# Attention inside the chunk: two row groups in turns instead of one after the other

## The reference, cut to what matters

```python
def step(S, inp):
    q_t, k_t, v_t, beta_t = inp
    retrieval = jnp.einsum('bhij,bhj->bhi', S, k_t)
    S = S + jnp.einsum('bhi,bhj->bhij', beta_t * (v_t - retrieval), k_t)
    o_t = jnp.einsum('bhij,bhj->bhi', S, q_t)
    return (S, o_t)
```

## Time and profile before

| | us |
|---|---|
| median of 3 runs | 1087.6 |
| lowest and highest | 1085.69, 1088.12 |
| the profiled execution | 1085.21 |
| its span, first to last instruction | 1083.3 |
| mean granted clock of TensorE | 0.927 |

### The profile page before, as it was taken

One profiled execution on the slowest core, in us unless ns is written; L12 is line 12 of the kernel. 1 busy time (PEld: TensorE's weight loads), 2 busy tenths in 40 slices (PEclk: granted clock), 3 DMA queues, 4 the chain that ended last, 5 costly groups with the idle time before them and its releaser, 6 DMA issues.

```text
span 1083.3 us, 19506 instructions
## 1 busy us (share of the span) xinstructions
PE 917.9 (85%) x6091; PEld 697.9 (64%) x6091; DVE 912.3 (84%) x2731; ACT 651.2 (60%) x1574; POOL 478.6 (44%) x667
## 2 busy tenths in 40 slices
PE   7799999999999999999999989899797701796066
PEld 7577887878787787787787776666565500343044
DVE  5789999989999999999999997665676788699887
ACT  4566676657667766666666643556667431695085
POOL 4444464455456545445345352316467550780000
PEclk9899999999999999999999999999999855798579
DMA  9600000000000000003000000214200000000012
GB/s 167 121 5 7 6 11 7 7 7 9 6 6 11 7 6 11 6 6 128 6 7 10 7 7 10 89 59 143 90 1 1 1 0 0 1 1 1 1 59 97
DMA packets 28573, 30.49 MB, mean 28 GB/s; under 512 B 5548, under 2 KB 23864, under 8 KB 28472
## 3 DMA queue, kind: packets, MB, share of 16 engines
q1 hardware_dynamic: 28256, 29.12, 10.5%
q10 hardware_dynamic: 216, 0.14, 0.0%
HBM read 20.85 MB, written 4.19 MB: 23 GB/s over the span
## 4 chain that ended last, share of the span: by engine, by line
PE 71%; DVE 21%; issue 5%; ACT 1%; DMA 1%; SPq 1%; POOL 0%; DVEq 0%; ACTq 0%; POOLq 0%
PE ps L1867 7%; PE ps L1859 7%; PE ps L1798 5%; PE psG L1821 5%; PE psY L1835 5%; PE psX L1835 4%; PE ps L1979 4%; PE psX L1913 3%; PE psY L2000 3%; PE psY L1913 3%; PE psG L1815 3%; PE psX L2000 2%; PE ps L1927 2%; PE ps L2165 2%; PE psG L1979 2%
## 5 line engine op out<-in xcount | busy, mean ns | idle before, releaser
L521 POOL TENSOR_TENSOR arena<-arena 128x256 f32<-128x256 f32 x32 | 23.3, 729 | 308.5 <-DVE arena L1147 300.9
L626 ACT ACTIVATE arena<-ps 128x512 f32<-128x512 f32 x128 | 72.9, 596 | 39.8 <-PE ps L1859 39.4
L1859 PE MATMUL ps<-work 32*128 32x256 f32 x512 | 93.7, 405 | 3.3 <-ACT work L672 2.3
L489 POOL TENSOR_SCALAR_AFFINE_SELECT arena<-arena 128x2048 f32<-128x2048 f32 x32 | 92.1, 2880 | 2.2
L591 ACT ACTIVATE arena<-ps,nparity 32x256 f32<-32x256 f32 x124 | 51.2, 459 | 48.7 <-PE ps L1798 48.3
L1859 PEld LDWEIGHTS ps<-work 32*128 32x128 f32 x512 | 62.2, 186 | 20.3 <-issue 12.5
L1821 PE MATMUL psG<-arena 128*128 128x512 f32 x128 | 73.2, 657 | 0.0
L1158 DVE TENSOR_TENSOR arena<-arena 128x256 f32<-128x256 f32 (+1 forms) x96 | 66.8, 696 | 3.3
L1798 PE MATMUL ps<-work,arena 128*128 128x64 f32 x496 | 63.2, 283 | 6.7 <-DVE work L1173 6.6
L1161 DVE TENSOR_REDUCE arena<-arena 128x64 f32<-128x256 f32 (+1 forms) x96 | 65.9, 687 | 3.3
L1835 PEld LDWEIGHTS psY<-work,arena 128*128 128x128 f32 x512 | 58.7, 192 | 12.6 <-DVE arena L1230 11.6
(11 more groups left out here) (349 smaller groups left out, 2604.3 us busy)
## 6 DMA issues: line engine op xcount, KB each, us to landing
arena<-in_mask_BxSxS_ik SPq DMA_DIRECT2D x8, 1024.0 KB, 7.2
xs<-arena SPq DMA_DIRECT2D x256, 16.0 KB, 1.8
arena<-in_ctx SPq DMA_DIRECT2D x8, 512.0 KB, 4.2
out<-xs SPq DMA_DIRECT2D x32, 128.0 KB, 1.7
arena<-in_x SPq DMA_DIRECT2D x8, 288.0 KB, 16.8
arena<-in_L_ffn_w SPq DMA_DIRECT2D x2, 1024.0 KB, 22.7
arena<-in_x SPq DMA_DIRECT2D x16, 96.0 KB, 5.7
arena<-in_L_attn_w_qkvb SPq DMA_DIRECT2D x2, 512.0 KB, 4.5
```

Source lines behind the costliest of these rows:

```text
L489: G.affine_select(out=pairs, in_=pairs, compare_op=ALU.is_ge, fill=0.0, base=0, pattern=[[0, NH], [-CT, B], [0, CT]], channel_multiplier=1 ...
L626: A.activation(attn[j % 2][:, r * 512:(r + 1) * 512], ps[(2, 0)[r % 2]][:, :], ACT.Copy).then_inc(att_out, 1)
L1859: last = M.matmul(ps[(2, 0)[r % 2]][:, f * 2 * P:(f + 1) * 2 * P], kq[j % 4][rows, f * P:(f + 1) * P], qe[rows, f].rearrange("p e t -> p ( ...
```

## The change

`attention` is now called once per pair of groups, `attention(j, f)` with pair 0 (groups 0 and 1) and pair 1 (groups 2 and 3). Inside, f is the outer loop and the two groups the inner one, so that the matmuls alternate between groups and banks. The waits of a pair all stand before its first matmul: `ust_ready` is waited for before group 0 also, and pair 1 waits until both evictions of pair 0 are done. Each group still raises `att_mm` after its last matmul.

```diff
-            def attention(j, r):
-                if r == 0:
+            def attention(j, pair):
+                if pair == 0:
                     pe.wait_ge(qe_ready, j + 1)
                     if j >= 1:
                         pe.wait_ge(x_done, j - 1)
-                elif r == 1:
                     pe.wait_ge(ust_ready, j)
                 else:
-                    pe.wait_ge(att_out, 4 * j + r - 1)
-                rows = slice(32 * r, 32 * r + 32)
+                    pe.wait_ge(att_out, 4 * j + 2)
                 for f in range(DC):
-                    last = M.matmul(ps[(2, 0)[r % 2]][:, f * 2 * P:(f + 1) * 2 * P], kq[j % 4][rows, f * P:(f + 1) * P],
-                                    qe[rows, f].rearrange("p e t -> p (e t)"), start=True, stop=True)
-                last.then_inc(att_mm, 1)
+                    for r in (2 * pair, 2 * pair + 1):
+                        rows = slice(32 * r, 32 * r + 32)
+                        last = M.matmul(ps[(2, 0)[r % 2]][:, f * 2 * P:(f + 1) * 2 * P], kq[j % 4][rows, f * P:(f + 1) * P],
+                                        qe[rows, f].rearrange("p e t -> p (e t)"), start=True, stop=True)
+                        if f == DC - 1:
+                            last.then_inc(att_mm, 1)
...
                 for f in range(2):
                     if exists(j):
-                        attention(j, 2 * f)
-                        attention(j, 2 * f + 1)
+                        attention(j, f)
```

## The result

| | before | after |
|---|---|---|
| median, us | 1086.4 of 20 runs | 1090.8 of 20 runs |
| lowest and highest | 1079.25, 1090.91 | 1084.01, 1092.65 |
| the profiled execution | 1085.21 | 1091.96 |
| its span | 1083.3 | 1090.1 |
| mean granted clock of TensorE | 0.927 | 0.925 |

The ratio of after to before is 1.0032, with a 95% interval of 1.0018 to 1.0046: 3.5 us more, between 2.0 and 5.0. The means of the two sets of 20 runs, 1086.2 and 1089.7, differ by the same 3.5. The change makes the kernel slower by a third of a per cent.

The account below looks back on a forecast made before the run. TensorE's unbroken line was taken to set a steady chunk's time. The wait's 1.9 us plus 0.5 in chunk 31 gave 2.4, so 1087.6 for the profiled execution and 1090.0 on the median; range 1087.0 to 1092.6.

Parts of the forecast that it names:

- Part 1: Attention matmuls in turns: row groups already run side by side, so the new order gains nothing and costs zero.
- Part 2: The ust_ready wait ahead of group 0 becomes its own instruction: 0.08 us later per chunk, 1.9 us over 24 chunks.
- The upper bound of 0.08: First pair's delay per chunk, bounded 0.01 to 0.08 us; the top assumes the load starts 0.11 after L608 ends.
- The bare shift: Group 0 losing its 0.60 us head start in the first pair: nothing, since group 1 set the pair's end; 0.01 per chunk.
- Part 3: Second pair waits for both evictions: covered, by 0.05 us only, by far gram and turned norms; costs where cover is missing.
- Chunk 31: Last chunk, nothing between the pairs: second pair's later group starts 0.54 us late; carried as 0.5, bounds 0.1 and 1.1.
- A: Rival, 4%: first pair shrinks to the second's form, 0.59 us in 24 chunks, 14.2 in all: 1073.4.
- B: Rival, 16%: the ust_ready wait ahead of the first pair is free; 0.7 us left, 1088.3, no measurable change.
- C: Rival, 9%: cover between the pairs fails, second pair starts 0.07 us late in 24 chunks: 1.7 more, 1091.7.
- D: Rival, 11%: idling before the first pair lowers TensorE's clock, 1.6 us a stretch: one fall 1091.6, every fifth chunk 1098.

Follow-up runs that it names:

- e9: The kernel before with VectorE's solve step t = 8 left out from chunk 1 on: ratio to before 0.9895, chunk 20.213 us.
- e4: The changed kernel with ust_ready named in the middle of the three waits and x_done last: ratio to before 1.0038, chunk 20.262 us.
- e5: The changed kernel with a fourth, long-met wait (k_ready) named last, making two wait instructions: ratio to before 1.0070, chunk 20.413 us.
- e1: The changed kernel's alternating matmuls, but each group's wait stays ahead of its own first matmul as before: ratio to before 1.0014, chunk 20.207 us.
- e2: The kernel before, matmuls still group by group, but with the waits of the change: ratio to before 1.0021, chunk 20.320 us.
- e3: The changed kernel with ust_ready named first of the three waits, so it rides on the weight load: ratio to before 1.0000, chunk 20.213 us.
- e7: The changed kernel with both halves of the far gram moved behind the second pair: ratio to before 1.0382, chunk 21.10 us.
- e6: The kernel before with both halves of the far gram moved behind the second pair: ratio to before 1.0103, chunk 20.545 us.
- e8: The kernel before with the far gram's first half ahead of the first pair, the second between the pairs: ratio to before 1.0004, chunk 20.184 us.
- e11: The kernel before with the retrieval's first two waits exchanged, so ScalarE's sexp_act is named first: ratio to before 0.9997, chunk 20.196 us.

## Why the prediction was right, and where it wasn't

Predicted were 1090.0, a range of 1087.0 to 1092.6, and slower as the likeliest. The ratio gives 1087.6 × 1.0032 = 1091.1, and the median of after is 1090.8. That 1090.0 lies only 0.8 under it is partly luck: the predicted difference of 2.4 was 1.1 under the measured 3.5, and the median of three runs that it was added to was 1.2 above the median of 20.

**What bounds the kernel.** Right: e9 shortens VectorE and the steady chunk doesn't move, while what is added ahead of the first pair comes out in the chunk within 3 ns: against group 1's 808 ns in before, attention starts 46, 91 and 197 ns later in e4, after and e5, and the chunk grows by 49, 94 and 200.

**Part 1, turns cost and bring nothing.** Right, by e1: 20.207 against 20.213. The Trainium skill's page "TensorE: Matmul & The Clock Gate" (Part 3, "The mechanism") has matmuls start and end in strict program order. The prediction set against it, but these are weight loads and don't settle how matmuls go. The matmul records do. In the second pair of before, and in both pairs of e2, all four records of one group stand ahead of the other's in the program, and yet the later group's first starts 13 or 14 ns after the earlier group's first. In the first pair of before, group 0's last record starts 147 ns after group 1's first (each group's records are told by their spacing of 216 ns). Here the trace and the page part. In turns (e1) the groups start 7 ns apart, and the pair takes the same 1.13 or 1.14.

**Part 2, the form of the wait.** Right in mechanism, and close in size. The load comes 0.11 after L608's end, as the earlier trace rows had it, and that it is the form and not the wait is shown by e3, e4 and e5: 0.05, 0.07, 0.11 and 0.22 us for the same release, by how it is named. The text left open whether `ust_ready` would share an instruction with `x_done`. It does, and still costs 0.11, while the earlier trace rows and e4 have 0.07 for such an instruction. The difference is which of the two is named last: in after it is the late one, in e4 and the earlier trace rows a fulfilled one. That the condition named last is looked at first, so that `x_done` has still to be gone through in after, would fit, and so do the 2.6 us of e4's wait instruction against 51 ns in after; no run shows the inside of that instruction. Per chunk it was 0.093 where 0.08 was predicted: 2.2 us instead of 1.9. The upper bound of 0.08 was too low by 0.013: the load comes 0.063 later (0.113 against 0.050 behind L608), and the first matmul's own lag behind its load, which grows from 0.00 to 0.03, was left out. The bare shift, taken as 0.01 from rows rounded to hundredths, is nothing in e3 and hid part of that.

**Part 3, cover.** Right: no pause ahead of the second pair in after, with 418.53 against an eviction that ends at 418.42. e7 gives the price with no cover, 0.56 a chunk before the clock joins in. Chunk 31 was foreseen at 0.54 and measured 0.7. The step holds (the later group starts 0.54 later), and the term is short by what follows it: from the later group's start to the outputs were 679.88 − 678.40 = 1.48 us and are 686.76 − 685.13 = 1.63, as both groups' records, not only the later one's, now fall where TensorE's clock is on its way down (in after, 685.10 to 686.80, next row; in the earlier trace rows the same drop). That was put into the bounds instead of the term. Where the clock is full throughout, the last chunk takes 3.79 us from L1809 to the outputs in e6 and 4.35 in e7, 0.56 apart: the predicted term.

```profile
685.10:686.80 1.70, 1.67 (x9) 0.91 (x10) 1.56 (x5) 0.47 (x1) 0.00 (x0) 0.64 0.52 154
```

Of the stretch of 1.70 us TensorE was busy for 1.67, at a granted clock of 0.64.

**The sum.** 2.9 instead of 2.4 from the traces, 3.2 ± 0.4 at equal clock, 3.5 by the ratio: the three agree within their errors. The 4.4 between the medians is 0.9 more than the 3.5 between the means. The half-clock stretches make a run longer or shorter by several us and stand in the prediction's range, not in its sum.

**The rivals.** A (−14.2) could not have come true even with a short first pair and no wait: e8 builds that and the chunk stays at 20.18. Its price was wrong, since it took 0.59 off TensorE's line in 24 chunks without asking how late VectorE is. The earlier trace rows held the hint: in a sixth interval L1798 started 0.05 after L1173's end, so the two were level there. The right price was 0.03 a chunk, 0.7 us, and A would have been a case of no change. B (the wait is free) is what e3 makes of the kernel by moving one line: a ratio of 1.0000 [0.9985, 1.0015]. The forecast and B lay one line of source apart. C didn't come: the two evictions of the first pair take 1.09 us together, as those of the second pair do, where the earlier trace rows had 1.20. D didn't come in after: the pause of 0.62 in every chunk brings no half-clock stretch in mid-loop. Its price was right: the stretches of e7, in about every third chunk, cost 1.65 us each, close to the 1.6 that the prediction put on one. That pauses bring them is not shown, as e6 has one where TensorE hardly paused. The parts of the chances add up to 0.08 for faster and 0.54 for slower, where the prediction has 0.07 and 0.55.

## What to carry to other kernels

Where several waits stand ahead of one TensorE instruction, name the one that comes last first, so that it rides on the instruction: on a path without slack the form of the wait cost 0.02 (e11's retrieval) to 0.20 us (e5) in every chunk here. Before reordering matmuls for overlap, look whether the weight loads and matmuls of two row groups already begin together somewhere in the trace; if they do, the stagger elsewhere is a semaphore, and merging waits can only move the early group to the late one. And price a gain only up to the point at which the next engine is late: read its distance at the place where the loop closes.

## What the runs showed of the hardware

- From the end of ScalarE's copy to TensorE's first weight load: 0.05 us when the wait is on the load, 0.07 when it is one condition of a two-condition wait instruction and the other, fulfilled one is named after it, 0.11 when the late one is named last, 0.22 with one wait instruction more. A satisfied wait instruction on this queue is not free.
- Matmuls of two row groups run side by side in either order of writing, at 7 ns (in turns) or 13 to 14 ns (in a row) between the groups' records.
- A wait instruction that was there before its last condition is recorded for as long as it stood (2.6 us in e4) or for 51 ns only (after), by the order in which its two conditions are named.
- Runs of one and the same kernel differ by stretches of some 3.4 us at half clock (0.50 of full, 1.2 GHz), which makes the mean granted clock of a run worth recording: 0.9 us for each 0.001. By plain ratio e4 is as slow as after; by chunk length and at equal clock it costs about half of it, and no run says what lowered the clock of its runs.
- A stretch of 3.40 us with one pause of 0.67 (2.69 busy) was followed by half clock in e7, and one with a pause of 0.75 (2.65 busy) in e6, where a like pause at 321 was not; the single pause of 0.62 per chunk in after was not, in the 14 chunks between 326 and 611.
